# The experts stages of a fourteen-stage network: the first layer's weights copied by POOL, two tiles ahead, and the first bias read in place

## The reference, cut to what matters

```python
# L0: top 1, tanh-gelu, no biases
h = gelu(einsum('td,edh->teh', xf, w1)); y = einsum('teh,ehd->ted', h, w2)
out = einsum('te,ted->td', one_hot, y)
# L1: top 2, weighted, biases b1 and b2
h = gelu(xt @ W1[e] + b1[e]) @ W2[e] + b2[e]
out = out + combine[:, e:e + 1] * h
```

## Time and profile before

| what | value |
|---|---|
| median of 3 runs | 4944.28 us (4939.39 to 4946.53) |
| the profiled execution: span, first to last instruction | 4944.1 us |
| the same execution's time beyond its span | not given apart; the span lies 0.2 us under the median of the runs |
| busy: PE, DVE, ACT, POOL | 78%, 70%, 47%, 48% |
| mean granted TensorE clock | 0.900 |
| indirect DMAs of y (L1434) | 220, 213.7 us |
| copies to W1s (L1645) | 220, median 604 ns, 426 to 2011 |

### The profile page before, as it was taken

How to read it: one execution, slowest core, us unless ns; L and a number is a source line. 1 busy time by engine, 2 the same in 40 slices (tenths; PEclk the granted TensorE clock), 3 DMA queues, 4 the chain that set the end, 5 groups by cost and what they waited for, 6 DMA issues and landing times. The chain is left out here.

```text
span 4944.1 us, 90876 instructions
## 1 busy us (share of the span) xinstructions
PE 3835.4 (78%) x25840; PEld 2735.3 (55%) x25840; DVE 3465.1 (70%) x9524; ACT 2341.8 (47%) x5537; POOL 2386.9 (48%) x3900
## 2 busy tenths in 40 slices
PE   7889797779999799568869937567775887799365
PEld 5666565656666466456646626422332665466265
DVE  7887775666666676566658856669998664588566
ACT  3444464355666466234436624345553454366243
POOL 5666442534344442446643354367776662233453
PEclk9999898789999899679979959779998999899698
DMA  6000332100000232133323311212121330133113
GB/s 234 0 0 1 112 124 76 52 20 1 0 0 1 72 124 94 39 124 107 107 80 117 110 38 47 73 48 65 63 62 64 114 117 28 51 120 112 36 46 87
DMA packets 244547, 341.24 MB, mean 69 GB/s; under 512 B 26976, under 2 KB 187120, under 8 KB 243120
## 3 DMA queue, kind: packets, MB, share of 16 engines
q1 hardware_dynamic: 230960, 309.19, 18.8%
q0 software_dynamic: 13184, 27.22, 1.6%
HBM read 182.77 MB, written 147.26 MB: 67 GB/s over the span
## 5 line engine op out<-in xcount | busy, mean ns | idle before, releaser
L522 DVE TENSOR_REDUCE l0att_rowmax<-l0att_S 128x2 f32<-128x512 f32 x512 | 339.8, 687 | 125.2 <-PE l0att_S L701 122.9
L893 POOL TENSOR_TENSOR wb_prob<-wb_prob,wb_rden 128x128 f32<-128x128 f32 (+1 forms) x512 | 248.2, 506 | 360.7 <-DVE wb_rden L1070 360.3
L522 DVE TENSOR_REDUCE l1ffn_rowmax<-l1ffn_S 128x2 f32<-128x512 f32 x512 | 337.6, 686 | 87.2 <-PE l1ffn_S L701 83.1
L1983 POOL TENSOR_TENSOR ssm_hc<-core_AW_all,ssm_Cs 128x512 f32<-128x512 f32 x256 | 320.8, 1268 | 131.2 <-DVE core_AW_all L2129 98.1
L1434 POOL DMA_INDIRECT results<-e_y,e_back x220 | 213.7, 971 | 289.4 <-DVE e_y L1662 269.9
L935 ACT ACTIVATE wb_prob<-wb_biased,wb_nmax 128x128 f32<-128x128 f32 (+1 forms) x512 | 228.6, 447 | 236.0 <-DVE wb_nmax L1063 233.6
L2228 PE MATMUL ssm_Y<-ssm_hc,core_ident 128*128 128x512 f32 x512 | 287.8, 672 | 56.8 <-POOL ssm_hc L1983 31.1
L2129 DVE TENSOR_TENSOR_SCAN core_AW_all<-core_AW_all,ssm_U 128x512 f32<-128x512 f32 x256 | 310.6, 1213 | 1.0 <-ACT core_AW_all L2072 0.6
L701 PE MATMUL l1ffn_S<-l1ffn_K,l1ffn_Q 128*128 128x512 f32 x512 | 251.0, 494 | 75.1 <-DVE l1ffn_rowmax L522 42.3
L1775 PE MATMUL e_H<-e_xT,e_W1s 128*128 128x128 f32 x1760 | 252.0, 288 | 70.2 <-issue 50.6
L701 PE MATMUL l0att_S<-l0att_K,l0att_Q 128*128 128x512 f32 x512 | 248.6, 489 | 60.4 <-DMA l0att_K<-bounce 47.5
(11 more groups left out here) (498 smaller groups left out, 11511.3 us busy)
## 6 DMA issues: line engine op xcount, KB each, us to landing
bounce<-l0att_parts SPq DMA_DIRECT2D x128, 256.0 KB, 2.8
bounce<-l1ffn_parts SPq DMA_DIRECT2D x128, 256.0 KB, 2.8
ssm_Cs<-c_rows SPq DMA_DIRECT2D x128, 256.0 KB, 3.1
routed<-core_Y SPq DMA_DIRECT2D x8, 2048.0 KB, 24.8
l0att_Q<-bounce SPq DMA_DIRECT2D x128, 128.0 KB
l0att_K<-bounce SPq DMA_DIRECT2D x128, 128.0 KB
bounce<-l1att_parts SPq DMA_DIRECT2D x64, 256.0 KB, 2.8
l1ffn_Q<-bounce SPq DMA_DIRECT2D x128, 128.0 KB
```

The lines of the kernel that those rows point to most:

```text
L522: dve.tensor_reduce(out=rowmax[:, jp, qt, 2 * pair:2 * pair + 2], in_=S[a % 2][:].rearrange("p (j k) -> p j k", j=2)[:, :, 0:keys(qt)], op ...
L893: ins = pool.tensor_tensor(out=prob[:, w_ % NP, a:b], in0=prob[:, w_ % NP, a:b], in1=rden[:, w_ % NP, n:n + 1].to_broadcast([P, b - a]), o ...
L1983: pool.tensor_tensor(out=hc[:, u % 4], in0=hs[:, u % 4], in1=Cs[:, n % 4], op=ALU.mult)\
```

## The change

POOL makes the weight copies, into a ring of three; it copies for tiles 0 and 1 ahead of its loop and for tile j+2 at the head of step j. VectorE keeps a register load only where b2 is added. ScalarE reads b1 in place, at an address from a register of its own. TensorE's register load stands behind the first layer.

```diff
-        W1s = sb("W1s", [P, 2, FC * P])
-        b1s = sb("b1s", [P, 3, FC]) if b1 is not None else None
+        W1s = sb("W1s", [P, 3, FC * P])
...
+            def weights(j):
+                e = pool.value_load(expert_i[0:1, j:j + 1], min_val=0, max_val=E - 1)
+                await_(pool, hid_made, j - 2)
+                pool.tensor_copy(W1s[:, j % 3], core.W1[:, bass.ds(e, 1), :].rearrange("p o f -> p (o f)"))\
+                    .then_inc(w1_copied.sem, 1)
+
+            pool.wait_ge(w_loaded[0], w_loaded[1])
+            pool.wait_ge(offsets_made.sem, 1)
+            weights(0)
+            weights(1)
             steps = 0
             for j in range(NT):
+                if j + 2 < NT:
+                    weights(j + 2)
                 pool.wait_ge(y_taken.sem, j + 1)
                 pool.wait_ge(back_ready.sem, j + 1)
...
             def activate(j):
+                e = expert.pop(j, None)
                 act.wait_ge(hid_made.sem, j + 1)
...
-                    act.wait_ge(w1_copied.sem, j + 1)
                     for f in range(FC):
                         ins = act.activation(hidden[:, j % 2, f], H[j % 2][:, f * P:(f + 1) * P], act_fn,
-                                             bias=b1s[:, j % 3, f:f + 1])
+                                             bias=b1[:, bass.ds(e * FC + f, 1)])
...
+            if b1 is not None:
+                act.wait_ge(offsets_made.sem, 1)
             for j in range(NT + 1):
                 if j < NT:
                     features(j)
+                    if b1 is not None:
+                        expert[j] = act.value_load(expert_i[0:1, j:j + 1], min_val=0, max_val=E - 1)
...
-            def weights(j):
-                e = expert[j] = dve.value_load(expert_i[0:1, j:j + 1], min_val=0, max_val=E - 1)
-                await_(dve, hid_made, j - 1)
-                if b1 is not None:
-                    await_(dve, acted, j - 2)
-                    step(dve.tensor_copy(b1s[:, j % 3], core.b1[:].rearrange("p (e f) -> p e f", e=E)
-                                         [:, bass.ds(e, 1), :].rearrange("p o f -> p (o f)")))
-                    settle()
-                dve.tensor_copy(W1s[:, j % 2], core.W1[:, bass.ds(e, 1), :].rearrange("p o f -> p (o f)"))\
-                    .then_inc(w1_copied.sem, 1)
...
-            dve.wait_ge(w_loaded[0], w_loaded[1])
...
-            for j in range(NT + 2):
-                if j < NT:
-                    weights(j)
-                if j >= 2:
-                    give(j - 2)
+            for j in range(NT):
+                if b2 is not None:
+                    expert[j] = dve.value_load(expert_i[0:1, j:j + 1], min_val=0, max_val=E - 1)
+                give(j)
...
             pe.wait_ge(offsets_made.sem, 1)
+            pe.wait_ge(w_loaded[0], w_loaded[1])
             for j in range(NT + 2):
                 if j < NT:
                     turn(j)
-                    expert[j] = pe.value_load(expert_i[0:1, j:j + 1], min_val=0, max_val=E - 1)
                 if 1 <= j <= NT:
                     hidden_layer(j - 1)
+                if j < NT:
+                    expert[j] = pe.value_load(expert_i[0:1, j:j + 1], min_val=0, max_val=E - 1)
                 if j >= 2:
                     output(j - 2)
```

More of the change, by code:

```diff
@@ L1341, in experts @@
         x_made, x_taken = sig("x_made"), sig("x_taken")
-        w1_copied, hid_made, acted, y_made, y_taken, back_ready = (
-            sig("w1_copied"), sig("hid_made"), sig("acted"), sig("y_made"), sig("y_taken"),
-            sig("back_ready"))
+        w1_copied = sig("w1_copied")
+        hid_made, acted, y_made, y_taken, back_ready = (
+            sig("hid_made"), sig("acted"), sig("y_made"), sig("y_taken"), sig("back_ready"))
         given = sig("given")
@@ L1480, in features @@
                     act.activation(xT[:, j % 2], F[j % 2][:, 0:P], ACT.Copy).then_inc(x_taken.sem, 1)
+            expert = {}
             def activate(j):
+                e = expert.pop(j, None)
                 act.wait_ge(hid_made.sem, j + 1)
@@ L1658, in give @@
                     dve.tensor_tensor(out=biased[:, j % 2], in0=YB[j % 2][:, 0:D],
-                                      in1=b2_all[:, bass.ds(expert[j], 1), :].rearrange("p o d -> p (o d)"),
+                                      in1=b2_all[:, bass.ds(expert.pop(j), 1), :].rearrange("p o d -> p (o d)"),
                                       op=ALU.add).then_inc(given.sem, 1)
@@ L1774, in hidden_layer @@
                 for f in range(FC):
-                    ins = pe.matmul(H[j % 2][:, f * P:(f + 1) * P], W1s[:, j % 2, f * P:(f + 1) * P], xT[:, j % 2],
+                    ins = pe.matmul(H[j % 2][:, f * P:(f + 1) * P], W1s[:, j % 3, f * P:(f + 1) * P], xT[:, j % 2],
                                     start=True, stop=True)
```

## The result

The changed kernel takes 5062.88 us in the median of 4 runs (5059.05 to 5064.72); the kernel before, run beside it on the same chip, takes 4941.84 us (4938.68 to 4946.53). The ratio is 1.0239, 95% interval 1.0224 to 1.0253. The forecast was 5006, slower; the sign is right, the size is half: 62 us were forecast, 119 measured between the profiled spans.

What follows compares the result with a forecast made beforehand. VectorE was taken to bound the 71-tile stages, TensorE the 39-tile ones; POOL's new loop and additions add 21.7, 23.1, 8.8 and 8.3 us, together +62 on 4944.1, giving 5006 us. Range of 8 in 10: 4960 to 5078.

Steps and rivals of the forecast that it cites:

- Step (c): POOL's queue: copy for tile j+3 behind tile j's scatter DMA; two-tile loop of 4.39 us (39-tile stages), 4.65 us (71-tile).
- Step (e): ScalarE, 71-tile stages: 1.94 of 2.33 us, costs nothing; TensorE's moved register load: covered, if late up to 21 us.
- the bare register load: Rival: POOL's register load uncovered on every tile, 55 us more, 5061 us; chance 0.15.
- the long copy: Rival: POOL's weight copy takes near 1.27 us, 5075 us; chance 0.08, shared with TensorE's load coming late.
- POOL's parallel cores: Rival: copy and load run beside DMA and additions, 4916 us, chance 0.07; loop part alone 4941, within a 0.08 case.
- the shared port: Rival: POOL's copy holds up VectorE's index operations in the 71-tile loop, 0.62 us a tile, 5094 at most; chance 0.05.
- Step (d): POOL, every fourth tile: additions into X ahead of the copy lengthen the loop by 2.07 us (39-tile stages), 3.47 (71-tile).
- the sum: Tile loops from third tile to last first layer: 96.4 us per 39-tile stage, 186.7 per 71-tile stage, together +62 us.
- "Nothing else can move": Claim that only the tile loops of the four experts stages, together 525 us, can change.

Runs made afterwards that it cites:

- e2: Changed kernel with a ring of four weight buffers and POOL's copies three tiles ahead: 4937.63 us, ratio 0.9985 to the kernel before.
- e7: Changed kernel with POOL making each weight copy twice, once into a spare buffer nobody reads: 5140.37 us, ratio 1.0395 to the kernel before.
- e4: Kernel before with only the bias part: ScalarE reads b1 in place, VectorE still copies the weights: 4900.71 us, ratio 0.9911.
- e5: Changed kernel with VectorE's index operations put ahead of its register load in the 71-tile stages: 5059.81 us, ratio 1.0243 to the kernel before.
- e8: Changed kernel with sixteen idle matmuls before the first layers that wait for additions in the 71-tile stages: 5045.57 us, ratio 1.0211 to the kernel before.
- e1: Changed kernel with VectorE's program in the 39-tile stages made as long as before by unused instructions: 5049.11 us, ratio 1.0209 to the kernel before.
- e6: Kernel of e4 with VectorE's weight copies one tile earlier, into a ring of three: 4862.65 us, ratio 0.9843 to the kernel before.

## Why the prediction was right, and where its size failed

**Right: the mechanism and its place.** Step (c), the loop from y over the scatter DMA and the copy to the next but one first layer, is the cause. In the 39-tile stages it runs at 4.39 us, as forecast to the hundredth; e2 breaks it with one more buffer, and 125 us are gained; e7 lengthens it by 0.56 and pays for it in each loop. The two unknown prices were right: the copy takes 0.62 us (0.61 forecast, from the earlier trace rows), and the register load on POOL is hidden behind the DMA and bare, 0.82 us, behind an addition (0.80 forecast). Step (e) held for ScalarE (e4); for TensorE the second layer starts 0.97 us behind the first, as before (3173.07, 3174.04), so its moved register load isn't late there, which no run tested by itself. The rivals of the bare register load, the long copy and POOL's parallel cores fell with these rows; the shared port is real in single rows, but e5, which removes most of its catches, gains nothing that can be measured.

**Step (d), the additions: right in length, priced without the clock.** 3.46 us from DMA to copy against 3.50. But the step priced only the wait itself. TensorE stands still about 4 us, and the granted clock is then at 0.5: 1.7 us more before the next b2 addition (3.89 against 2.17) at each of some eight places per stage. The error is 25 us in e8's two 71-tile stages, the largest single term in them. In the 39-tile stages the half-clock time rose from 5.8 and 4.8 us to 9.9 and 15.9, and the two stages lie 1.4 and 4.9 us above the sum. No run removed it there, but the groups show it: the five groups in which such a stretch falls take 11.9 to 12.3 us, the others 10.9 to 11.2. Executions of the same stage code agree: 10.1 us at half clock and 103.2 us of stage in e5's second, 15.8 and 106.1 in e8's first.

**Step (c) in the 71-tile stages: 4.65 for what takes about 4.81.** The sum used the 1.09 us of the 39-tile loop from second layer to VectorE; with b2's address computed behind the wait it is 1.20 (e5). DMA and copy took 0.98 and 0.62 for 0.96 and 0.61. These make 0.14; the plain loop of e5 is 0.16 longer than the sum, in 34 loops 5.4 us a stage, 11 in both. With the clock that makes 36 of the 39 us by which the two stages exceed the sum; the rest fits port catches, which was not separated.

**"Nothing else can move" was wrong.** 17.8 us came between the first two stages, in a loop that the change does not touch, by the code of VectorE ahead of it (e1): about 12.7 us in five returns to the loop's top, where code was fetched anew, and 4.9 in three stretches at half clock. The other stretches gave back 6.0. Net 11.8 of the 57 us missed.

**The range held**, but by the width that the rivals gave it (to 5078): no case in it was the clock or the code, which together are 37 of the 57 us missed (25.5 in the 71-tile stages and, net, 11.8 between the stages).

## What to carry to other kernels

"n tiles ahead" is no distance if the copy stands in a queue behind work that waits for a recent result: write the loop out, divide it by the tiles it spans, and buy one more buffer before moving work to another engine. Here the same order of copies is faster on the old engine each time: two tiles ahead by 162 us (e4 against the kernel after), three tiles ahead by 75 (e6 against e2), some 18 of each in the wide loop. A wait of a few us on TensorE should be priced with the clock behind it, and a change of the number of instructions ahead of a loop in the program can move that loop.

## What the runs showed of the hardware

- TensorE's granted clock was 0.50 behind waits of about 4 us in the tile loop, and in three of five cases behind a wait of some 2 us in the wide attention. Sixteen idle matmuls in each wait of the 71-tile stages held it at 1.00, and that alone made the kernel 17 us faster (e8).
- A loop in the program ran 17.6 us longer in six turns. At each of its five returns VectorE's sequencer lost some 2.5 us (2.72 to 2.87 in place of 0.25), with 25 packets of code fetched where there had been none, and e1's extra instructions in a stage ahead of it removed both.
- POOL's copy of 128x512 f32 takes 0.62 us (0.56 from start to start where two follow each other, e7) and begins within 0.01 us of the end of the indirect DMA ahead of it (1003.43 + 0.98, 1004.41).
- VectorE's 128x1 operation took 1.97 us from 3121.12, although POOL's addition begins only at 3121.79 by its row. It lasts up to that addition's end (3123.06), and without a hold it takes 0.16 us, so it was held before 3121.28, while POOL's row is still that of its indirect DMA. The Trainium skill (SBUF — State Buffer, SBUF: two separate sides) says of the shared port pair that the loser waits out the whole instruction; by that the end agrees. The start is not explained by it, since VectorE's row is the earlier one, and no run here shows when the hold is taken.
